# Sixteen tables instead of fourteen looked up by one-hot matmuls, in a one-core recommendation kernel

## What is computed

```python
e = jnp.stack([tbl_0[ids[:, 0]], ..., tbl_25[ids[:, 25]]], axis=1)          # 512 x 26 x 128
combined = concatenate([dense[:, None, :], e], axis=1)                      # 512 x 27 x 128
interactions = einsum('bfd,bgd->bfg', combined, combined)[:, iu, ju]        # upper triangle, 351
z = concatenate([dense, interactions], axis=1)
h = concatenate([z, dense], axis=1)
h = maximum(h @ W_top1 + b_top1, 0)      # 512 wide
h = maximum(h @ W_top2 + b_top2, 0)      # 256 wide
y = h @ W_top3
```

## Time and profile before

| | |
|---|---|
| median of three runs | 122.68 us (122.09 to 122.89) |
| the profiled execution's own time | 122.1 us |
| its span, first to last instruction | 119.9 us |
| PE busy | 105.5 us, 88% |
| DVE and ACT busy | 83.5 us, 82.2 us |
| POOL busy | 62.8 us, the last gather issued at 78.2 us |
| lookup stage | 5.8 to 69.8 us |
| second stage | 69.8 to 119.9 us |

### The profile page before, as it was taken

The page is one execution under the profiler, slowest core; times in us unless marked ns, Lnnn a source line. Parts: engine busy times, 40 slices in busy tenths (PEclk is TensorE's granted clock), DMA queues, the critical chain, the costliest instruction groups (busy, mean ns, idle before and its releaser), DMA issues.

```text
span 119.9 us, 3695 instructions
## 1 busy us (share of the span) xinstructions
PE 105.5 (88%) x1541; PEld 88.1 (73%) x1541; DVE 83.5 (70%) x198; ACT 82.2 (69%) x149; POOL 62.8 (52%) x56
## 2 busy tenths in 40 slices
PE   0299699998899997995997999977999999999993
PEld 0076588876788685883885888766998989999971
DVE  2569999989869979979949242396398485485110
ACT  5676999999999999999956050675393492492131
POOL 3777788787777887878777767730000000000000
DMA  2699889988648677768941112210000000000000
GB/s 84 163 333 386 304 269 259 358 284 249 200 149 288 195 237 276 264 213 202 409 135 44 51 44 60 60 49 0 5 5 8 5 5 0 5 3 5 0 0 1
DMA packets 6452, 16.81 MB, mean 140 GB/s; under 512 B 1570, under 2 KB 1570, under 8 KB 6308
## 3 DMA queue, kind: packets, MB, share of 16 engines
q1 hardware_dynamic: 4898, 13.43, 33.8%
q0 software_dynamic: 1536, 3.15, 8.7%
q10 hardware_dynamic: 2, 0.00, 0.0%
HBM read 16.57 MB, written 0.00 MB: 138 GB/s over the span
## 4 chain that ended last, share of the span: by engine, by line
PE 72%; DVE 19%; issue 5%; DMA 1%; ACT 1%; DVEq 0%
PE gram_ps L572 17%; PE gram_ps L574 15%; DVE onehot L488 13%; PE gram_ps L609 10%; PE h_ps L634 10%; DVE table_lo L494 5%; PE h_ps L648 5%; PE fill_ps L585 4%; PE gram_ps L634 3%; PE h_ps L624 3%; PE h_ps L661 2%; PE fill_ps L677 2%; DMA ids_row<-oh_ids 1%; PE gram_ps L624 1%; PE h_ps L684 1%
## 5 line engine op out<-in xcount | busy, mean ns | idle before, releaser
L318 POOL DMA_INDIRECT gathered<-tbl,ids_sb x48 | 62.0, 1291 | 15.7 <-issue 14.3
L572 PE MATMUL gram_ps<-onehot,table_hi 128*128 128x512 f32 x116 | 47.4, 409 | 7.8 <-DVE table_lo L494 4.2
L574 PE MATMUL gram_ps<-onehot,table_lo 128*128 128x512 f32 x116 | 46.5, 401 | 0.0
L488 DVE TENSOR_SCALAR onehot<-ids_all,rowno 128x512 fp32r<-128x512 int32 x93 | 38.9, 485 | 7.2 <-PE gram_ps L574 4.6
L572 PEld LDWEIGHTS gram_ps<-onehot,table_hi 128*128 128x128 f32 x116 | 22.6, 195 | 15.2 <-issue 9.5
L574 PEld LDWEIGHTS gram_ps<-onehot,table_lo 128*128 128x128 f32 x116 | 22.6, 195 | 4.5
L494 DVE TENSOR_TENSOR table_lo<-table_sb,table_hi 128x1024 fp32r<-128x1024 f32 (+1 forms) x13 | 16.3, 1255 | 0.9 <-ACT table_hi L385 0.9
L347 ACT ACTIVATE zT<-gram_ps 32x128 f32<-32x128 f32 x32 | 8.6, 270 | 10.8 <-PE gram_ps L609 10.1
L458 DVE COPY zT<-gram_ps 32x128 f32<-32x128 f32 x32 | 9.0, 283 | 9.4 <-PE gram_ps L609 8.5
L406 ACT ACTIVATE onehot<-ids_all,minus_rowno 128x512 fp32r<-128x512 int32 x23 | 15.4, 712 | 0.0
L385 ACT ACTIVATE table_hi<-table_sb 128x1024 fp32r<-128x1024 f32 (+1 forms) x13 | 14.0, 1077 | 1.9 <-DMA table_sb<-tbl 1.9
(11 more groups left out here) (48 smaller groups left out, 64.2 us busy)
## 6 DMA issues: line engine op xcount, KB each, us to landing
table_sb<-tbl SPq DMA_DIRECT2D x11, 512.0 KB, 4.7
ids_all<-oh_ids SPq DMA_DIRECT2D x13, 256.0 KB, 4.9
table_sb<-tbl SPq DMA_DIRECT2D x2, 640.0 KB, 4.1
w_inter_sb<-w_inter SPq DMA_DIRECT2D x1, 1024.0 KB, 8.4
gathered<-tbl,ids_sb POOLq DMA_INDIRECT x48, 4.6
table_sb<-tbl SPq DMA_DIRECT2D x2, 256.0 KB, 3.1
w_dense_sb<-w_dense SPq DMA_DIRECT2D x1, 512.0 KB, 6.0
w_sb<-w SPq DMA_DIRECT2D x1, 512.0 KB, 9.4
```

Source lines behind the costliest of these rows:

```text
L318: pool.indirect_dma_start(out=gathered[:, t % ROW_BUFS, pos - FIRST_GATHERED, :], out_offset=None, in_=tables[table], in_offset=bass.Indir ...
L488: nc.vector.tensor_scalar(onehot[k % 2][:, c, :], ids_all[:, k % IDS_BUFS, :], row_number(rowno, k, c), None, ALU.is_equal).then_inc(oneho ...
L572: nc.tensor.matmul(lookup_ps(k), table_hi[k % SPLIT_BUFS][:, rows], onehot[k % 2][:, c, :], start=(c == 0), stop=False)
L574: last = nc.tensor.matmul(lookup_ps(k), table_lo[k % SPLIT_BUFS][:, rows], onehot[k % 2][:, c, :], start=False, stop=(c == row_chunks(k) - 1))
```

## The change

- `ONEHOT_TABLES` has 16 tables instead of 14; the two new ones (21 and 22) are LONG. Lookups go from 232 matmuls to 272. Gathered are ten tables, 40 gathers, in groups of 4, 4 and 2 slots; tile 0's groups are transposed behind lookups 4, 6 and 8 instead of 2, 4 and 6.
- Behind each gather POOL has a memset of a 128x320 scratch tile; each memset waits for the one before it.
- `ids_all` has two rows for each buffer, the ids and the ids plus one. ACT makes the second row (`next_ids`). DVE's compare covers two chunks in one instruction (`compare_two`).
- DVE makes all 8 chunks of an even SHORT table (k > 0), 6 of an odd one, 8 of a LONG one. ACT makes the last two for table 0 and for odd k, and none for even k above 0. All four LONG tables are at odd k.
- DVE's order is low parts, then compares. ACT's is Abs and Relu, the next table's ids plus one, its high parts, then the rest as before.
- `PAIR_SLOTS` are chosen anew: both slots of a pair lie in one aligned block of four slots, but for the last pair, which is copied slot by slot. The gathered groups begin at slots 12, 16 and 20.
- `h1` and `h2` lie in table buffers. The order of fills, products and layers in the second stage is changed in places: one fill fewer ahead of `products(0, 0)`, fills in twos, `layer2(1)` and `layer2(2)` moved.

```diff
-ONEHOT_TABLES = (0, 1, 3, 6, 8, 7, 11, 12, 14, 15, 16, 13, 18, 20)
-LARGER = (7, 13)
+ONEHOT_TABLES = (0, 1, 3, 6, 8, 7, 11, 13, 12, 14, 15, 21, 16, 22, 18, 20)
+LARGER = (7, 13, 21, 22)
+PAUSE = 320
-PAIR_SLOTS = ((4, 7), (9, 10), (0, 1), (3, 5), (6, 8), (11, 12), (13, 14))
+PAIR_SLOTS = ((4, 7), (9, 10), (0, 1), (5, 6), (8, 11), (24, 25), (22, 23), (3, 26))
-FIRST_GATHERED = 1 + ONEHOTS
+FIRST_GATHERED = 3 * GROUP
+GATHERED = SPARSE - ONEHOTS
-AFTER_LOOKUP = [[], [], [(0, 0)], [], [(0, 1)], [], [(0, 2)], [], [], [], [], [], [], []]
+AFTER_LOOKUP = [[], [], [], [], [(0, 0)], [], [(0, 1)], [], [(0, 2)], [], [], [], [], [], [], []]
...
-    return LONG - 2 if row_chunks(k) == LONG else 6 + k % 2
+    if row_chunks(k) == LONG:
+        return LONG - 2
+    return SHORT if k > 0 and k % 2 == 0 else SHORT - 2
...
+        h1 = table_sb[1][:, 0:2 * N1 * P].rearrange("p (t n b) -> p t n b", t=2, n=N1)
+        h2 = table_sb[0][:, 0:N2 * BATCH].rearrange("p (n b) -> p n b", n=N2)
...
+                        if pauses > 0:
+                            pool.wait_ge(paused, pauses)
+                        pool.memset(scratch[:, :], 0.0).then_inc(paused, 1)
+                        pauses += 1
...
+            def compare_last(k):
+                if k == 0:
+                    act.wait_ge(ids_0_ready, 1)
+                if k >= 2:
+                    act.wait_ge(lookup_done, k - 1)
+                for c in range(dve_chunks(k), row_chunks(k)):
+                    nc.scalar.activation(onehot[k % 2][:, c, :], ids_all[:, k % IDS_BUFS, 1, :], ACT.Abs,
+                                         bias=row_number(minus_rowno, k, c)).then_inc(id_off_ready, 1)
+                ...
+            def next_ids(k):
+                act.wait_ge(ids_all_in[k % IDS_BUFS], ids_loads(k))
+                nc.scalar.activation(ids_all[:, k % IDS_BUFS, 0, :], ids_all[:, k % IDS_BUFS, 1, :], ACT.Relu, bias=1.0) \
+                    .then_inc(next_ids_ready, 1)
...
             for k in range(ONEHOTS):
+                if dve_chunks(k) < row_chunks(k):
+                    compare_last(k)
+                if k + 1 < ONEHOTS:
+                    next_ids(k + 1)
                 if k + 1 < ONEHOTS:
                     high_parts(k + 1)
...
+            def compare_two(k, c):
+                nc.vector.tensor_scalar(onehot[k % 2][:, c:c + 2, :], ids_all[:, k % IDS_BUFS, :, :],
+                                        row_number(rowno, k, c + 1), None, ALU.is_equal).then_inc(onehot_dve, 2)
...
                 if k > 0:
-                    dve.wait_ge(ids_all_in[k % IDS_BUFS], ids_loads(k))
+                    low_parts(k)
+                    dve.wait_ge(next_ids_ready, k)
...
-                    for c in range(dve_chunks(k)):
-                        compare(k, c)
-                    low_parts(k)
+                    for c in range(0, dve_chunks(k), 2):
+                        compare_two(k, c)
...
             fill(1, 0)
-            fill(1, 1)
             products(0, 0)
             products(0, 1)
+            layer1_dense(1)
+            fill(1, 1)
             fill(1, 2)
             products(0, 2)
-            layer1_dense(1)
             fill(2, 0)
             products(0, 3)
             fill(2, 1)
+            fill(2, 2)
             products(1, 0)
-            fill(2, 2)
             layer1_dense(0)
             products(1, 1)
             fill(3, 0)
+            fill(3, 1)
             products(1, 2)
-            fill(3, 1)
             layer1(0, 0)
...
```

More of the change, by code:

```diff
@@ L119, in tower @@
         dense_sb = sb("dense_sb", [P, TILES, DIM])
-        gathered = sb("gathered", [P, ROW_BUFS, FEATS - FIRST_GATHERED, DIM])
+        gathered = sb("gathered", [P, ROW_BUFS, GATHERED, DIM])
         featT = sb("featT", [P, BATCH, SLOTS])
@@ L391, in _ @@
             act.wait_ge(ids_0_psum, 1)
-            nc.scalar.activation(ids_all[:, 0, :], h1_ps[:, :], ACT.Copy).then_inc(ids_0_ready, 1)
+            nc.scalar.activation(ids_all[:, 0, 1, :], h1_ps[:, :], ACT.Copy).then_inc(ids_0_ready, 1)
             act.wait_ge(table_0_in, 16)
@@ L398, in _ @@
             for k in range(ONEHOTS):
-                if k > 0:
-                    act.wait_ge(ids_all_in[k % IDS_BUFS], ids_loads(k))
-                else:
-                    act.wait_ge(ids_0_ready, 1)
-                if k >= 2:
-                    act.wait_ge(lookup_done, k - 1)
-                for c in range(dve_chunks(k), row_chunks(k)):
-                    nc.scalar.activation(onehot[k % 2][:, c, :], ids_all[:, k % IDS_BUFS, :], ACT.Abs,
-                                         bias=row_number(minus_rowno, k, c)).then_inc(id_off_ready, 1)
-                act.wait_ge(id_off_ready, act_chunks_to(k + 1))
-                act_part = onehot[k % 2][:, dve_chunks(k):row_chunks(k), :]
-                nc.scalar.activation(act_part, act_part.bitcast(fp32), ACT.Relu, bias=1.0, scale=-1.0) \
-                    .then_inc(onehot_act, row_chunks(k) - dve_chunks(k))
+                if dve_chunks(k) < row_chunks(k):
+                    compare_last(k)
+                if k + 1 < ONEHOTS:
+                    next_ids(k + 1)
                 if k + 1 < ONEHOTS:
@@ L518, in _ @@
                 if k == 0:
-                    for c in range(2):
-                        compare(0, c)
+                    compare_0(0)
+                    compare_0(1)
                     low_parts_0(0)
-                    compare(0, 2)
-                    compare(0, 3)
+                    compare_0(2)
+                    compare_0(3)
                     low_parts_0(1)
                     for c in range(4, dve_chunks(0)):
-                        compare(0, c)
+                        compare_0(c)
                 else:
-                    for c in range(dve_chunks(k)):
-                        compare(k, c)
-                    low_parts(k)
+                    for c in range(0, dve_chunks(k), 2):
+                        compare_two(k, c)
             last_but_one_lookup_to_featT()
@@ L727, in _ @@
             products(LAST, 1)
+            layer1(1, 3)
+            layer1_dense(LAST)
+            products(LAST, 2)
             layer1_dense(2)
-            layer1(1, 3)
-            products(LAST, 2)
-            layer1_dense(LAST)
             products(LAST, 3)
-            layer2(1)
             layer1(2, 0)
@@ L736, in _ @@
             layer1(2, 2)
+            layer2(1)
             layer1(2, 3)
```

29 lines of the change are left out of this document (18 added, 11 removed).

## The result

| | kernel before | kernel after |
|---|---|---|
| median of 4 runs, us | 122.39 (121.52 to 122.89) | 131.55 (130.49 to 132.28) |
| ratio to before | 1 | 1.0768, 95% interval 1.071 to 1.0826 |
| profiled execution, us | 122.1 | 131.94 |
| its span, us | 119.9 | 130.1 |
| end of the last lookup, us | 69.78 | 79.50 |

The change makes the kernel 7.7% slower. The prediction was 127.0 us with a range from 122.3 to 130.5: the direction was right, the time is 4.5 us above it and 1 us above its range.

The account below looks back on a forecast made before the run. PE, DVE and ACT were taken as nearly full in the lookups, PE alone as the second stage's chain, POOL as not binding. Lookups to 75.2 plus 49.6 gave 124.8, plus 2.2 around the span 127.0 us; range 122.3 to 130.5.

Parts of the forecast that it names:

- Matmuls: PE in the lookups: 40 more matmuls at 0.227 us each add 9.1 us.
- The walk through the three engines: Lookups followed table by table on PE, DVE and ACT: 1.9 us lost by table 6, last lookup ends at 75.2.
- The memset: Behind each gather: could hold DVE's compares up to 0.3 us each, 7 us in all; 0 put in the sum.
- POOL: Gathers with memsets: period 2.05 us under the lookups, 38th gather begins at 80, tile 3's last group not late.
- Rival 3's other arm: Late gathers of tile 3, from a POOL period of about 2.25 us on: up to 133 us; whole rival's chance 0.15.
- The compare of two chunks: DVE in the lookups: 0.66 us each, length 0.74; at 0.79 PE would lose 3.5 us in all.
- ids ahead of the high parts on ACT: Lookups: ids loads land 1.2 us late at tables 9 and 13, costing nothing, up to 1.5 us if loads are slower.
- Aligned slots: ACT's pair copies: all near 1.1 us; three no longer lie across two blocks, which takes back 3 x 0.8 us.
- The second stage: After the lookups: 49.6 us, 0.7 less for transposes, 0.2 more for one fill fewer, both old gaps kept.
- rival 2: Second stage: the two gaps in the products vanish, 1.7 us, with no lookup waits left: 122.9 us; chance 0.12.
- PE bound: Lookups: no wait of PE is left, 72.8 us for the lookups, 124.6 in all; chance 0.18 alone.
- The memset's hold on DVE: Lookups: memsets lock DVE out during compares, adding 3.5 us for 130.5; chance 0.15 together with late gathers.

Follow-up runs that it names:

- e1: The kernel after without the memset behind the gathers, nothing else changed; 127.71 us, ratio 1.0469 to the kernel before.
- e7: e1 with one compare for each chunk and without the ids plus one on ACT; 127.68 us, ratio 1.0484 to the kernel before.
- e5: e1 with the second stage in the order of the kernel before on PE, ACT and DVE; 126.78 us, ratio 1.0463 to the kernel before.
- g11: e1 with eight waits on a long-raised semaphore behind each lookup in PE's program, shifting later code; 149.14 us on a disturbed chip.
- e6: e1 with 14 one-hot tables and 48 gathers instead of 16 tables; 117.70 us, ratio 0.9701 to the kernel before.
- h1: The same kernel as e6, run once more; 118.04 us, ratio 0.969 to the kernel before.
- e4: The kernel before with a 128x320 memset behind each of its 48 gathers; 128.79 us, ratio 1.048 to the kernel before.

## Why the prediction was right in direction and wrong in size

**Matmuls.** 40 more at 0.227 us: right. The median distance in e1 is 0.227, and e1 ends where the sum with this count says. In the kernel after it is 0.231.

**The walk through the three engines.** Right to 0.4 us at every table from 1 to 6: predicted 13.4, 17.5, 21.1, 25.4, 29.65, 35.3; e1 has 13.06, 17.16, 20.90, 25.40, 29.69, 35.29; end 75.2 against 75.51. A walk over rows of the old trace was good enough for a kernel in another order.

**The memset: the step that failed.** "I put 0 in the sum and 3.5 at the top of the range." The mechanism was named, with a rule and a row for it, and so was the size: 35 x 2/3 x 0.3 = 7 us of DVE, half of it absorbed. Measured are some 21 met compares at 0.43, 9.1 us of DVE, and 4.0 in the time. The estimate was a quarter low on DVE and an eighth on the time; what went wrong is that a cost with a mechanism, a count and a price was left out of the sum because only one half of the rule had a row. With 3.5 in it the sum would have been 130.5, its range's top; the 1.1 us above that are for the most part the half us by which the memset was priced too low, and the second stage. The row that it had, gathers lengthened among compares, couldn't have told more: in e1, among 40 gathers, no compare takes over 0.82 us, so gathers wait for compares and hold them by 0.08 at most, where a memset of 0.39 holds them by 0.43. For such a cost a chance of 0.15 was low.

**POOL.** Predicted period 2.05 us, measured (69.67 - 2.8) / 39 = 1.72. Two terms: the memset takes the place of part of the pause before a gather, which is 0.16 to 0.17 us now and was 0.30; and gathers are shorter than before, 1.17 us on average for 1.29. The prediction had the 38th gather begin at 80; by its own period it would be 2.8 + 37 x 2.05 = 78.7. It began at 65.9 and the last at 69.7, so tile 3's are in time by far. Rival 3's other arm, late gathers, was wrong.

**The compare of two chunks.** Price right: 0.66 from start to start, 0.74 long, once the memsets are away. Its worth was not: the prediction says that at 0.79 PE would lose 3.5 us, and e7, where a pair of chunks does take 0.79, loses nothing. At the same time ACT is relieved of 0.53 us a table, and the early tables begin up to 1.9 us sooner for it. That bound was taken on one engine alone.

**ids ahead of the high parts on ACT.** Predicted were waits of ACT of 1.2 us at tables 9 and 13 that PE doesn't feel, and "up to 1.5 us if loads are slower". The waits of the kernel after (total, times, longest):

```profile
ACT ids_all L415 <- DMA ids_all<-oh_ids: 6.9, 5, 2.4
```

That is more than said. In e1 they are 4.3 us (0.5 at table 9, 0.9 at 13, and others at tables 1, 3 and 15), and e1 still ends where the sum has it. So ACT had the room for it in e1. How much of the 6.9 is paid for in the kernel after wasn't separated from the memset; the ids wait for the compares of three tables before, which the memset makes late, so part of it is the same cost seen from ACT.

**Aligned slots.** Right: seven copies of 1149 ns on average, none over 1161.

**The second stage.** 50.6 for 49.6, a term that was too small as well: the pauses grew from 1.7 to 3.4 us, where the sum kept 1.7. It had them as something that might vanish (rival 2) and not as something that might double. That is the smaller part of the miss, and it isn't explained beyond what is said of e5 and g11.

**Rivals.** PE bound (124.6) fell: the waits at tables 4 and 6 are there in e1. The vanishing gaps came true only at 14 tables, and in part (0.6 us left in e6, 1.2 in h1). The memset's hold on DVE is the one that held.

## What to carry to other kernels

When a change puts GpSimd work beside a DVE that is nearly full, look which of DVE's instructions it holds (here the compares, not the low parts), count the GpSimd instructions that fall into those, price each at its own length, let about half through to the time (0.37 to 0.57 of it here), and put that into the sum. Before trading a gather for one-hot work, see that PE has the time: two tables cost some 9 us in the lookups here, and the gathers that they replaced had cost none. What paid was an order, the operand that everything waits for (the low parts) ahead of the compares, worth 3.8 us.

## What was not expected of the hardware

- A memset of 0.39 us on POOL lengthens the compare that it meets by 0.43 us, one of 0.65 by 0.70, and one of 0.14 by at most 0.09; in return a memset of 0.14 us takes 0.56 to 0.58 under a compare. The subtraction that makes the low parts takes 1.21 us with and without a memset in it.
- A gather's length changes with what DVE and POOL do around it: 1.05 us on average among compares of 0.74 (e1), 1.65 among compares of 0.48 that do the same work (e7). With memsets between the gathers it is the other way round, 1.17 (after) and 1.03 (e4).
- PE's pauses in streams of short matmuls (0.2 to 1.6 us each, up to 3.4 us in a kernel of 130) stand at fixed counts of PE's instructions, some 127 matmuls or a multiple of it apart but for single ones, whatever the matmuls compute. They move when the code is moved, and their size changes from run to run.
- On two chips with a lower granted clock, kernels that issued gathers back to back lost more time than one with a memset between them, one of them by standing still for 15 to 22 us at a time. That is an observation on two chips and has no cause here yet.
